# A transformer decoder block on one core: the angles in four pieces, the last quarter of the head outputs in two halves, residuals of batches 4 to 7 beside the first units

## The reference

```python
def block(x, ctx, pos):
    h = layernorm(x)
    # 1: 128 heads; q = [h Wq_down Wq_up | h Wq_rope], k = [h Wkv_down Wk_up | h Wk_rope]
    attn = softmax((q_c @ k_c.T + q_r @ k_r.T) / sqrt(4 + 64))
    x = x + concat_heads(attn @ v_c) @ Wo
    # 2: 32 query heads of 16, 8 key/value heads from ctx, rotated by the angles pos * inv_freq
    q, k = rope(layernorm(x) @ Wq), rope(ctx @ Wk)
    x = x + concat_heads(softmax(q @ k.T / 4) @ (ctx @ Wv)) @ Wo2
    # 3: dense layer, and two of eight rank-16 experts for each token
    return x + x @ base_w.T + base_b + 2 * mixture_of_low_rank(x)
```

## Time and profile before

| | us |
|---|---|
| median of three runs | 868.87 |
| lowest and highest | 867.58, 870.23 |
| the profiled execution | 867.85 |
| its span, from first to last instruction | 865.9 |
| PE busy | 803.9 (93%) |
| DVE busy | 647.9 (75%) |
| ACT busy | 568.5 (66%) |
| POOL busy | 582.8 (67%) |

### The profile page before, as it was taken

The page is one execution under the profiler, slowest core; times in us unless marked ns, Lnnn a source line. Parts: engine busy times, 40 slices in busy tenths (PEclk is TensorE's granted clock), DMA queues, the critical chain, the costliest instruction groups (busy, mean ns, idle before and its releaser), DMA issues.

```text
span 865.9 us, 17867 instructions
## 1 busy us (share of the span) xinstructions
PE 803.9 (93%) x5624; PEld 395.2 (46%) x5624; DVE 647.9 (75%) x1209; ACT 568.5 (66%) x1045; POOL 582.8 (67%) x492
## 2 busy tenths in 40 slices
PE   4999999999999999999999999999848688999986
PEld 3464444444454444444444444444313344555433
DVE  7866777767677888777888767788787567888754
ACT  4757777777777777777777777777530465555641
POOL 7747888888788878888888878885543223333210
PEclk9999999999999999999999999999978799999999
DMA  8344455434334332434333433432130000000001
GB/s 334 110 166 146 92 156 169 139 85 112 101 90 105 85 108 78 107 97 123 85 82 91 113 104 89 109 89 56 29 88 0 1 1 3 15 13 15 13 13 37
DMA packets 51227, 74.69 MB, mean 86 GB/s; under 512 B 9968, under 2 KB 33520, under 8 KB 50672
## 3 DMA queue, kind: packets, MB, share of 16 engines
q1 hardware_dynamic: 51184, 74.18, 30.7%
HBM read 38.16 MB, written 18.87 MB: 66 GB/s over the span
## 4 chain that ended last, share of the span: by engine, by line
PE 84%; DVE 8%; ACT 2%; issue 2%; DMA 1%; SPq 1%; POOL 0%; DVEq 0%; ACTq 0%
PE PS L1200 39%; PE PS L1152 8%; PE PS L1236 7%; PE PS L1266 6%; PE PS L1268 6%; PE PS L1283 5%; PE PS L1411 2%; PE PS L1325 1%; PE PS L1418 1%; PE PS L1380 1%; PE PS L1397 1%; PE PS L1426 1%; PE PS L1456 1%; DVE xm L1027 1%; PE PS L1244 1%
## 5 line engine op out<-in xcount | busy, mean ns | idle before, releaser
L492 POOL TENSOR_TENSOR Pl<-PR,Ph 128x512 f16<-128x512 f32 x254 | 285.8, 1157 | 24.7 <-ACT Ph L668 24.7
L661 ACT ACTIVATE PR<-PS 128x512 f32<-128x512 f32 x256 | 152.6, 597 | 135.0 <-PE PS L1268 128.5
L795 DVE TENSOR_REDUCE mneg<-PS 128x4 f32<-128x512 f32 x256 | 174.6, 684 | 38.2 <-PE PS L1236 34.7
L1200 PE MATMUL PS<-XTh,Wh 128*128 128x512 f16 x512 | 194.5, 380 | 0.0
L1200 PE MATMUL PS<-XTh,Wl 128*128 128x512 f16 x512 | 193.7, 378 | 0.0
L1200 PE MATMUL PS<-XTl,Wh 128*128 128x512 f16 x512 | 193.5, 378 | 0.0
L783 DVE SCALAR_TENSOR_TENSOR QS<-PS,QC 64x512 f16<-64x512 f32 x256 | 175.5, 686 | 18.0 <-ACT QC L593 10.9
L593 ACT ACTIVATE QC<-PS 64x512 f16<-64x512 f32 x256 | 150.7, 589 | 10.6 <-PE PS L1200 4.3
L668 ACT ACTIVATE Ph<-PR 128x512 f16<-128x512 f32 x256 | 139.3, 617 | 0.0
L474 POOL TENSOR_TENSOR Wh<-Wraw,wscale 128x1024 f16<-128x1024 f32 x32 | 60.6, 1893 | 70.8 <-PE PS L1200 67.5
L1236 PEld LDWEIGHTS PS<-KC,QC 112*128 112x128 f16 x1024 | 78.8, 97 | 62.2 <-issue 2.7
(11 more groups left out here) (213 smaller groups left out, 1163.4 us busy)
## 6 DMA issues: line engine op xcount, KB each, us to landing
Wraw<-in_wqr SPq DMA_DIRECT2D x32, 512.0 KB, 4.6
QS<-QC SPq DMA_DIRECT2D x64, 256.0 KB, 3.2
head_outputs<-OS SPq DMA_DIRECT2D x256, 40.0 KB
q_content_parts<-stg SPq DMA_DIRECT2D x12, 256.0 KB, 2.8
k_content_parts<-stg SPq DMA_DIRECT2D x12, 256.0 KB, 3.1
QC<-q_content_parts SPq DMA_DIRECT2D x128, 24.0 KB
KC<-k_content_parts SPq DMA_DIRECT2D x32, 96.0 KB
xs<-in_x SPq DMA_DIRECT2D x8, 256.0 KB, 4.5
```

Of the source, the lines that this page charges most:

```text
L492: nc.gpsimd.tensor_tensor(Pl[:, b], PR[:, b % 4], Ph[:, b], ALU.subtract).then_inc(s_pl, 1)
L661: nc.scalar.activation(PR[:, b % 4, :], PS[:, bB[b % 2], :], ACT.Exp, scale=ATT_SCALE).then_inc(s_e, 1)
L795: nc.vector.tensor_reduce(mneg[:, par, b // 4, :, b % 4], PS[:, bA[b % 2], :].rearrange("p (j k) -> p j k", j=GH), AX.X, ALU.max, negate=T ...
L1200: last = mm(PS[:, bQ[c % 2], :], wt[:, par, k, p * P:(p + 1) * P], xt[:, k, sl], start=(k == 0 and n == 0), stop=(k == KT - 1 and n == 2))
```

## The change

The order of the half steps stays as it is (the new table of jobs, `job` and `ago`, gives 0 to 63 in the old order at its values LG = 1, LATE = 62, TURN = 63), and `BY_DVE` is empty. The half steps of each engine are written as a function of the half step. In the main loop each projection has its products in another order with the same count. What else differs:

- `angles()` becomes four parts, one in each of half steps 22 to 25, between `o_out` and the row maxima.
- The contents of queries and keys for half steps 62 and 63 are loaded by half sizes (10 DMAs in place of 5), into an additional buffer `KC2`, which POOL fills with two copies at the start (3.9 us by the like copies of before).
- POOL makes all four `Pl` of half step 63. Its fills of `xvz`, `turns` (with the identity) and `kst` move into half steps 62 and 63.
- The last quarter is gathered in two halves of the batches: eight DMAs of half size once half step 62 is stored, then the loads of `lb_sb` and `bias`, the stores of half step 63 and eight further DMAs, which count on the semaphore `s_ue`.
- ACT's split of `Wxh` goes between half steps, and the other three into units 1, 2 and 3; DVE's low parts follow (`split_low`), the first before `o_out` of half step 61.
- In the loop over units DVE has: x1(1), k_rope(0) in unit -7; normalise of batch 2 and `o_out` of half step 63 in -6; normalise 3, x1(2) in -5; x1(3) in -4; normalise 4 and 5, x1(4), x1(5) in -1; split_low(1), normalise 6 in 1; split_low(2), k_rope(1), x1(6) in 2; split_low(3), normalise 7 in 3; x1(7) in 4.
- PE's outputs of quarters 0 to 2 for batches 0 to 5 are spread in the last half steps; those of the last quarter come in units -5 (batches 2, 3), -1 (4, 5) and 2 (6); batch 7 comes whole in unit 4. Unit -2 waits for x1 of batches 0 to 3 in place of all eight, and x_scores(0) for six.
- Buffers of the second and third step lie at other addresses of SBUF.

These wait for `u_norm`, which DVE's normalise of batch 7 raises in unit 3. The diff, cut to its core:

```diff
+LG = 1
+G0 = NG - LG
+LATE = NH - 2 * LG
+TURN = LATE + LG
...
+BY_DVE = range(LATE - 3, TURN - 4)
...
+            def half_quarter(t, j):
+                for s in range(2):
+                    sp.wait_ge(s_od[s], 64 * (NG if t else (TURN + 1 - s) // 2))
+                sp.wait_ge(s_un, B * (KT - 2) + B // 2 * (t + 1))
+                gather(KT - 1, j, t * B // 2, (t + 1) * B // 2, s_ue if t else s_ud[KT - 1])
...
+            outputs(job(NH - 3))
+            outputs(job(NH - 2))
             for j in range(GH):
-                gather(KT - 1, j)
-            sp.wait_ge(s_q, 4 * NG)
+                half_quarter(0, j)
+            sp.wait_ge(s_b, 4 * NH)
             sp.dma_start(lb_sb[:], lb).then_inc(s_ffn, 16)
             sp.dma_start(bias[:], bb.to_broadcast([P, DM])).then_inc(s_ffn, 16)
+            outputs(job(NH - 1))
+            for j in range(GH):
+                half_quarter(1, j)
             def x_maxima(u):
                 sp.wait_ge(s_xme, u + 1)
...
+                if u in (1, 2, 3):
+                    if u == 1:
+                        act.wait_ge(s_ffn, 48)
+                        act.wait_ge(s_pv, NH)
+                    split_high(u)
...
-                if g_is(g, NG):
-                    angles()
...
+                if h is not None and 22 <= h < 26:
+                    angles(h - 22)
...
+            def angles(part):
...
+                if part % 2 == 0:
...
-            k_rope(0)
-            k_rope(1)
-            normalise(KT - 1, 0)
-            normalise(KT - 1, 1)
...
+            split_low(0)
+            o_out(job(NH - 3))
+            o_out(job(NH - 2))
+            rope_factors()
+            normalise(KT - 1, 0)
+            normalise(KT - 1, 1)
             x1(0)
-            dve.wait_ge(s_x1, 1)
...
-                if u == FIRST:
+                if u == FIRST + 1:
+                    x1(1)
+                    k_rope(0)
+                if u == FIRST + 2:
                     normalise(KT - 1, 2)
-                    x1(1)
+                    o_out(job(NH - 1))
+                if u == FIRST + 3:
                     normalise(KT - 1, 3)
-                if u == FIRST + 1:
-                    normalise(KT - 1, 4)
                     x1(2)
-                if u == FIRST + 2:
-                    for v in range(3, EARLY):
-                        normalise(KT - 1, v + 2)
+                if u == FIRST + 4:
+                    x1(3)
+                if u == -1:
+                    for v in range(B // 2, EARLY):
+                        normalise(KT - 1, v)
+                    for v in range(B // 2, EARLY):
                         x1(v)
-                if u == FIRST + 5:
-                    for v in range(EARLY, B):
-                        x1(v)
-                    dve.wait_ge(s_x1, B)
+                if u in (1, 2, 3):
+                    split_low(u)
+                if u in (1, 3):
+                    normalise(KT - 1, 6 + u // 2)
+                if u == 2:
+                    k_rope(1)
+                if u in O1_AT:
+                    x1(O1_AT[u])
 
         @block.tensor
...
-                    pe.wait_ge(s_x1, B)
+                    pe.wait_ge(s_x1, B // 2)
+                    pe.wait_ge(s_kx, 2)
...
-                if u == FIRST + 2:
-                    for v in range(3, EARLY):
-                        output(v, KT - 1)
                 if u == FIRST + 3:
-                    for v in range(EARLY, B):
-                        pe.wait_ge(s_x1, v - EARLY + 1)
-                        for T in range(KT):
+                    output(2, KT - 1)
+                    output(3, KT - 1)
+                if u == FIRST + 4:
+                    pe.wait_ge(s_oe, NH)
+                    for T in range(KT - 1):
+                        output(EARLY, T)
+                if u in O1_AT:
+                    v = O1_AT[u]
+                    take(bF[1], s_x1, v + 1)
+                    for T in range(KT):
+                        if v > EARLY or T == KT - 1:
                             output(v, T)
                 if 0 <= u + 2 < NU:
                     x_rough(u + 2)
                 if 0 <= u + 1 < NU:
                     x_max_turn(u + 1)
+                if u == -1:
+                    output(4, KT - 1)
```

More of the change, by code:

```diff
@@ L1 @@
 import math
+from collections import namedtuple
 from contextlib import ExitStack
@@ L147, in build @@
         SU = sb("SU", [P, TOK])
+        KC2 = sb("KC2", [P, 2, TOK], F16)
+        assert top[0] <= end1
         assert end1 <= nc.sbuf_usable_end
@@ new lines, in p_high, with late_high @@
+            def p_high(j):
+                if later(j.n, 2):
+                    act.wait_ge(s_pv, j.n - 1)
+                for b in range(4):
+                    act.wait_ge(s_e, 4 * j.n + b + 1)
+                    nc.scalar.activation(Ph[:, 4 * j.s + b, :], PR[:, b, :], ACT.Copy).then_inc(s_ph, 1)
+            def late_high(g):
+                par = g % 2
+                act.wait_ge(s_w[par], 16 * (g // 2 + 1))
+                act.wait_ge(s_q, 2 * (LATE + g - 1 - G0))
+                if g == NG - 1:
+                    act.wait_ge(s_wst, 16)
+                nc.scalar.activation(Wh[:, par], Wraw[:, par], ACT.Copy, scale=WS).then_inc(s_wa, 1)
@@ new lines, in half @@
+            def half(g, par, t):
+                J = lambda d: ago(g, par, t, d)
+                if J(1) and later(J(1).n, 2):
+                    q_high(J(1), 1)
+                if isinstance(g, int) and LATE <= 2 * g + t < TURN - 1:
+                    late_high(J(0).g + 1)
+                if J(3):
+                    p_high(J(3))
+                for b in range(4):
+                    if J(2):
+                        exps(J(2), b)
+                    if b == 0:
+                        q_high(J(0), 0)
@@ new lines, in _, with split_high @@
+            spelled(half, 1, 2)
+            looped(act, half, 3, G0 - 1)
+            spelled(half, G0, NG - 1)
+            def split_high(n):
+                h, w = ((Wxh, wx_raw), (woh, xwo_sb), (bwh, bw_raw), (agh, ag_raw))[n]
+                nc.scalar.activation(h[:], w[:], ACT.Copy, scale=WS).then_inc(s_xh, 1)
+            q_high(job(NH - 1), 1)
+            p_high(job(NH - 3))
+            act.wait_ge(s_wx, 16)
+            act.wait_ge(s_q, 2 * NH)
+            split_high(0)
+            for n in (NH - 2, NH - 1):
+                for b in range(4):
+                    exps(job(n), b)
+                p_high(job(n))
@@ new lines, in half @@
+            def half(g, par, t):
+                J = lambda d: ago(g, par, t, d)
+                for n in range(8):
+                    project(J(0), n // KT, n % KT)
+                    if n == 0 and isinstance(g, int) and 2 * g + t == 2:
+                        pe.wait_ge(s_ul, 16)
+                        pe.wait_ge(s_vl, B)
+                        max_turn(job(0))
+                    if 1 <= n <= 4:
+                        rough_scores(J(1), n - 1)
+                    if 3 <= n <= 6:
+                        scores(J(2), n - 3)
+                    if n == 7:
+                        max_turn(J(1))
+                        if J(3):
+                            weigh(J(3))
@@ new lines, in _ @@
+            looped(pe, half, 3, G0 - 1)
+            spelled(half, G0, NG - 1)
+            pe.wait_ge(s_wo, 16)
+            for i in range(4):
+                rough_scores(job(NH - 1), i)
+                if i == 0:
+                    pe.wait_ge(s_ql, 4 * NH - 2)
+                if i < KT - 1:
+                    output(0, i)
+            pe.wait_ge(s_ql, 4 * NH)
+            for i in range(4):
+                scores(job(NH - 2), i)
+                if i < KT - 1:
+                    output(1, i)
+                if i == 0:
+                    max_turn(job(NH - 1))
@@ new lines, in _ @@
+            weigh(job(NH - 3))
+            pe.wait_ge(s_m, 4 * NH)
+            for T in range(KT - 1):
+                output(2, T)
+            for i in range(4):
+                scores(job(NH - 1), i)
+                if i < KT - 1:
+                    output(3, i)
+            weigh(job(NH - 2))
+            pe.wait_ge(s_e, 4 * NH)
+            for T in range(KT - 1):
+                output(4, T)
+            weigh(job(NH - 1))
+            for T in range(KT - 1):
+                output(5, T)
```

751 lines of the change are left out of this document (403 added, 348 removed).

## The result

The changed kernel takes 901.7 us in the median of four runs (901.2 to 902.9), the kernel before 868.8 in the same series: a ratio of 1.038, 95% interval 1.0361 to 1.0399. It is 3.8% slower. The profiled execution took 901.2 us with a span of 899.5, against 867.85 and 865.9.

The account below looks back on a forecast made before the run. PE, busy 93% of the span, was taken to bound the loop; behind it PE waits for others. Angles 14.9, clock 1.7, remaining gain -4.0 and units 1 to 4 12.4 make +25.0 on 867.85: 892.9, median 893.9, range 875 to 902.

Parts of the forecast that it names:

- three more clock losses: Upper end of the range: PE's other three stands in half steps 22 to 25 also lose 1.7 us each.
- a tail near 15: Upper end of the range: units 1 to 4 lose about 15 us in place of 12.4, with PE slower.
- 12.3 and 10: Lower end of the range: angles cost 12.3 us in place of 14.9, units 1 to 4 lose 10 for 12.4.
- The hold: Half steps 22 to 25: each small linked DVE operation ends when POOL's current one does; PE stands 14.9 us.
- the slack: In a loop half step, DVE's row maxima can come 0.45 us late before PE waits.
- The clock: After PE's stand of 5.25 us in half step 22, work is lost at a lower clock: 1.7 us, once.
- The gather: Last quarter: the first half lands at 639.5 in place of 646.36, 6.9 us earlier.
- the term of the twelve products: Between gather and first turn: the projection's twelve products run fully at the lower clock, 5.1 us, +2.5.
- Units -1 and 0: First turn to unit 2's turn: work of batches 4 and 5 adds 5.5 us, leaving 4.0 of the gain.
- Units 1 to 4: Unit 2's turn to unit 6's rough scores: added DVE work, walked in queue order, loses 12.4 us.
- The second rival: Angles are held, but units 1 to 4's extra work fills DVE's idle time, 1.3 lost: +13.9, 882.8 us; chance 0.20.
- The rival on the other side: Angles not held (2.4), first turn's 9.5 us lead kept through units -1 and 0, 1.3 lost later: 863.1; chance 0.08.

Follow-up runs that it names:

- The kernel at 863.7: Changed kernel with angles in idle gaps, splits and both k_rope before the units, half step 63's copy and batches 4 and 5's work earlier: 863.7 us, 0.9956 of the kernel before.

## Why the prediction was right, and where it was off

The forecast was 893.9 within 875 to 902, slower with 0.85; the measured 901.7 lies at the upper edge. By the spans the miss is 8.6 (+33.6 for +25.0): +5.3 in the half steps with the angles, +3.2 in two stretches put at nothing, +2.5 in units 1 to 4, +0.3 in units -1 and 0, and -2.7 on the way to the first turn, which hid a part of the others. The upper end of the range stood for three more clock losses and a tail near 15, and both came. Its lower end of 885 does not follow from the terms given for it: 12.3 and 10 make 888.9. Point by point:

- **The hold.** Right, and it is the largest term. The forecast stands were 5.25, 3.75, 2.2 and 3.7; PE's waits are 5.19, 3.37, 2.12 and 3.25, 13.9 for 14.9. The forms with a scalar and two tensors were taken as held, and they are: two in a row last 2.19. The Trainium skill ("SBUF — State Buffer", "Who interferes with whom") calls the pair of ports that VectorE and GpSimd share an exclusive lock; these rows, 0.20 or 1.82 for the same instruction, agree with it. Half of the difference of 1.0 lies in parts 1 and 3, which made the maxima 3.9 and 3.8 late where I had 4.2 and 4.15, since their first operation found POOL further on in its instruction; the other half is the slack, 0.57 and not 0.45.
- **The clock.** The term was mis-sized: 1.7 forecast, 8.0 measured. I let only the first stand count, since the other three were shorter than the 3.99 of the earlier trace rows, and put them in the range. Alone, a stand of 2.1 costs nearly nothing, as I had assumed; but here they follow one of 5.2 within four half steps, and then each costs 1.8 or more. The step that failed was to price each stand by its own length.
- **The gather.** Right: forecast landing 6.9 earlier relative to the loop, measured 8.0 (23.2 late at half step 25, 15.2 at the landing). Of this 1.1, 0.8 is a slip of mine: the landing of 2.19 counts from the issue of the fourth store, so three steps of 0.84 lie ahead of it and I added four. From landing to first turn, 21.2 against 22.8 forecast and 25.5 before; 0.8 of the difference is the term of the twelve products, 5.1 forecast and 4.35 measured. The rest lies behind them, 7.0 us where it was 8.0; the turn now waits there for output products and no longer for POOL.
- **Units -1 and 0.** Forecast +5.5, measured +5.8. The run with this work earlier showed that it was this work. But the agreement of the numbers is luck. I priced the two products of batches 4 and 5 at 1.6; they are four instructions of PE and took 3.78 at the lower clock. A rotation and one of the normalises stand ahead of them, which gave PE the wait of 4.43, and the residuals do not hold the turn. Against that, the twelve products of the projection took 2.75 where they took 4.40 before, a gain that I had not counted.
- **Units 1 to 4.** Forecast +12.4 by walking DVE's queue, measured +14.9. The rough scores of unit 6 came 35.8 after unit 2's turn where the walk had 33.3. The miss of 2.5 shows first at the rough scores of unit 4, 16.9 after the turn where the walk had 15.1, and again at the last product of batch 7, which took 2.07 after the wait of 3.95 where I had left 0.9. The second rival (the work falls into idle time, 1.3 lost) is refuted: the loss is larger than the 10.5 that DVE got. Splits and k_rope carried 7.3 of it (35.8 to 28.5), as the run without them showed. The last 7.6 I had put down to batches 6 and 7 by size; two runs speak against that.
- **What was at zero.** The start is 1.3 late. The ten kernels with this start lay between -0.1 and +2.1 against the one before, 1.2 in the mean, and the kernel before with only the angles moved at +0.5; so whether `KC2` costs anything there is not shown. The rest of the span, +1.9, has no cause that I tested. In the four other runs that leave units 1 to 31 as in the changed kernel it was 165.3, 167.0, 167.2 and 169.5, so 1.9 is no more than such kernels differ from each other; the kernel before has 165.0.

The rival on the other side, under 864 with the lead of the first turn kept, needed no hold and no work in units -1 to 4. The kernel at 863.7 comes out there by moving such pieces, but by another sum: it kept the lead of the first turn and still lost 6.9 in units 1 to 4 (27.8 for 20.9), where the rival had 1.3.

## What to carry to other kernels

A handful of tiny VectorE operations on SBUF, of the forms seen here, was free only where GpSimd was idle: beside a GpSimd instruction each lasted to that one's end, so look for a gap of both engines, not of VectorE alone. Work taken off a visible wait goes somewhere; put it where an engine stands for a transfer, not into a loop whose engines wait for each other step by step, even if that loop shows half of the time idle. And price stalls of TensorE in groups: here what followed soon after a long one cost more than its own length.

## What the runs showed of the hardware

The clock was the surprise. A stand of 10.2 us cost 2.0 beyond itself, one of 5.2 cost 2.4, one of 2.13 alone cost 0.2 with the granted clock at 1.00, and stands of 3.4, 2.1 and 3.3, each within 15 us of the one before, cost 1.8 to 1.9 each. And a reading of a timeline: in the run with the small `Pl` one and the same form took 0.22 us and, begun 0.26 us later, 1.82, by the one instruction that POOL had begun 0.13 us earlier.
